# A kernel of four fused layers: in the slots of routed experts, the low part of each prepared weight piece is stored one slot behind its high part, and the second weight load is issued two slots later

## The reference, cut to what matters

```
x = x + tanh(g_xattn[0]) * retention(layernorm(x), ctx)                      # stage 1
x = x + tanh(g_ffn[0])   * (routed(x') + shared(x'))        # x' = layernorm(x), stages 2 to 4
      logits = x' @ gate_w; the 2 best of 8 experts, softmax over the two
      routed: gelu(x' @ w1[e] + b1[e]) @ w2[e] + b2[e], weighted;  shared: the same form, all tokens
x = x + tanh(g_xattn[1]) * fp8_attention(layernorm(x), ctx, wq, wqx, wk, wv, w_kv_x, ...)  # stage 5
x = x + tanh(g_ffn[1])   * dense_ffn(layernorm(x), ...)                       # stage 6
```

## Time and profile before

| | |
|---|---|
| median of 3 runs | 1681.28 us (1679.48 to 1681.79) |
| the profiled execution's own time | 1685.41 us |
| its span, first to last instruction | 1683.7 us |
| mean granted TensorE clock | 0.993 |
| PE / PEld busy | 1626.0 us (97%) / 1334.5 us (79%) |
| DVE / ACT / POOL busy | 64% / 66% / 29% |
| DMA | 220.72 MB, mean 131 GB/s |
| the slots | from about 226 us to 398 us |

### The profile page before, as it was taken

One profiled execution on the slowest core, in us unless ns is written; L12 is line 12 of the kernel. 1 busy time (PEld: TensorE's weight loads), 2 busy tenths in 40 slices (PEclk: granted clock), 3 DMA queues, 4 the chain that ended last, 5 costly groups with the idle time before them and its releaser, 6 DMA issues.

```text
span 1683.7 us, 27163 instructions
## 1 busy us (share of the span) xinstructions
PE 1626.0 (97%) x9136; PEld 1334.5 (79%) x9136; DVE 1084.2 (64%) x2115; ACT 1105.8 (66%) x2983; POOL 488.2 (29%) x515
## 2 busy tenths in 40 slices
PE   7989979999999999999999999999999999999998
PEld 6878756666778888888888888788888788887887
DVE  6258845443996668777787776666666666788322
ACT  4364245553468988888888888787787787885100
POOL 1001123222524243343342432433433334331000
PEclk9999979999999999999999999999999999999999
DMA  7031638885773242373333353121152131110011
GB/s 270 26 107 51 256 133 299 302 302 177 262 238 119 82 161 84 132 294 125 132 139 130 132 224 121 56 89 56 49 201 102 39 113 56 38 45 1 25 38 38
DMA packets 75156, 220.72 MB, mean 131 GB/s; under 512 B 6368, under 2 KB 14560, under 8 KB 68640
## 3 DMA queue, kind: packets, MB, share of 16 engines
q1 hardware_dynamic: 69360, 200.61, 32.7%
q0 software_dynamic: 5680, 18.62, 3.6%
HBM read 158.65 MB, written 60.56 MB: 130 GB/s over the span
## 4 chain that ended last, share of the span: by engine, by line
PE 72%; DMA 6%; DVE 5%; ACT 4%; issue 1%; POOL 1%; ACTq 0%; DVEq 0%; POOLq 0%; SPq 0%
PE bank L2485 10%; PE bank L2486 10%; PE bank L2548 7%; PE bank L97 6%; PE bank L99 6%; PE bank L98 6%; PE bank L2566 6%; PE bank L2579 6%; DMA s_rows<-x_rows,t_tok 5%; PE bank L2537 5%; PE bank L2558 3%; PE bank L1396 2%; PE bank L1416 2%; DVE x_res L1754 1%; PE bank L1376 1%
## 5 line engine op out<-in xcount | busy, mean ns | idle before, releaser
L2817 DVE TENSOR_TENSOR t_hn<-bank,t_rs 128x256 f32<-128x256 f32 (+1 forms) x256 | 130.8, 553 | 138.7 <-POOL t_rs L2450 73.2
L2485 PE MATMUL bank<-t_slot,t_x_q 128*128 128x512 f32 x512 | 205.8, 402 | 0.0
L2447 POOL TENSOR_SCALAR t_ve<-t_ss 128x4 f32<-128x4 f32 (+1 forms) x128 | 26.1, 204 | 615.5 <-DVE t_ss L2813 608.0
L2486 PE MATMUL bank<-t_slot,t_x_q 128*128 128x512 f32 x512 | 200.3, 391 | 0.0
L2706 ACT ACTIVATE t_sc<-bank,t_mx 128x128 f32<-128x128 f32 x512 | 184.4, 456 | 3.2 <-DVE t_mx L2837 3.2
L2450 POOL TENSOR_TENSOR t_rs<-t_ve,t_mhalf 128x4 f32<-128x4 f32 (+1 forms) x128 | 171.2, 1337 | 10.7
L2706 ACT ACTIVATION_READ_ACCUMULATOR t_sc<-bank,t_mx 128x1 f32 x512 | 151.8, 296 | 0.0
L2744 ACT ACTIVATE t_y<-bank,smooth 128x128 bf16<-128x128 f32 x512 | 139.7, 402 | 1.9 <-PE bank L2566 1.9
L2548 PEld LDWEIGHTS bank<-t_hT 128*128 128x128 f32 x1024 | 120.0, 191 | 17.0 <-ACT t_hT L2733 16.5
L2548 PE MATMUL bank<-t_hT 128*128 128x128 f32 x1024 | 131.0, 281 | 2.3 <-ACT t_hT L2733 2.3
L2486 PE MATMUL bank<-t_slot,t_x_kv 128*128 128x256 f32 x512 | 125.6, 283 | 0.0
(11 more groups left out here) (344 smaller groups left out, 4165.5 us busy)
## 6 DMA issues: line engine op xcount, KB each, us to landing
t_slot<-w_ready SPq DMA_DIRECT2D x16, 2048.0 KB, 9.3
t_xh<-xq_scratch SPq DMA_DIRECT2D x64, 512.0 KB, 3.6
t_cr<-in_ctxT_dram SPq DMA_DIRECT2D x64, 256.0 KB, 2.7
y_rows<-s_y SPq DMA_DIRECT2D x39, 256.0 KB
e_w<-in_w_units_dram SPq DMA_DIRECT2D x8, 1024.0 KB, 12.2
w_rows<-in_w_qkv_dram SPq DMA_DIRECT2D x8, 1024.0 KB, 6.2
w_ready<-w_hi SPq DMA_DIRECT2D x8, 1024.0 KB, 5.0
w_ready<-w_lo SPq DMA_DIRECT2D x8, 1024.0 KB
```

The costliest lines, as they stand in the source:

```text
L2485: nc.tensor.matmul(out, x_in[:, k, :], w[0][:, k, a:b], start=k == 0, stop=False)
L2486: last = nc.tensor.matmul(out, x_in[:, k, :], w[1][:, k, a:b], start=False, stop=k == KT - 1)
L2817: nc.vector.tensor_tensor(hn[:, lo:hi, :], b3[bk][:, 0:hi - lo, :], rs[:, lo:hi].unsqueeze(2).broadcast_to([P, hi - lo, P]), ALU.mult).the ...
```

## The change

It touches only the order in which SP issues DMAs among the slots. No instruction of another engine changes.

- `store` is taken apart into `store_hi` and `store_lo`, which move from the subclass to the base class.
- The high part of piece n is stored behind the y store of slot 4n+4, as before. The low part is stored behind the y store of slot 4n+5.
- The load of piece 1 is taken from ahead of the slots and issued behind the y store of slot 2, by the same rule as the later pieces.

```diff
-    def store(self, sp, n):
-        quarter, k = self.where(n)
-        for part, (ready, tile, stored) in enumerate(((self.hi_in, self.hi, self.hi_st),
-                                                      (self.lo_in, self.lo[n % len(self.lo)], self.lo_st[n % 2]))):
-            sp.wait_ge(ready, n + 1)
-            sp.dma_start(self.dram[quarter, :, :, part, k, :].rearrange("s p n -> p s n"),
-                         tile[:].bitcast(FP32).rearrange("p (s n) -> p s n", s=4)).then_inc(stored, 16)
+    def store_hi(self, sp, n):
+        quarter, k = self.where(n)
+        sp.wait_ge(self.hi_in, n + 1)
+        sp.dma_start(self.dram[quarter, :, :, 0, k, :].rearrange("s p n -> p s n"),
+                     self.hi[:].bitcast(FP32).rearrange("p (s n) -> p s n", s=4)).then_inc(self.hi_st, 16)
+
+    def store_lo(self, sp, n):
+        quarter, k = self.where(n)
+        sp.wait_ge(self.lo_in, n + 1)
+        sp.dma_start(self.dram[quarter, :, :, 1, k, :].rearrange("s p n -> p s n"),
+                     self.lo[n % len(self.lo)][:].bitcast(FP32).rearrange("p (s n) -> p s n", s=4)).then_inc(self.lo_st[n % 2], 16)
...
         ready.load(sp, 0)
-        ready.load(sp, 1)
         for s in range(SLOTS_N):
             sp.wait_ge(self.y_in, s + 1)
             sp.dma_start(self.env.dram["y_rows"][s * P:(s + 1) * P, :], self.y[s % 2][:]).then_inc(self.y_st[s % 2], 16)
             if s % 4 == 0 and 0 < s // 4 <= ready.count:
-                ready.store(sp, s // 4 - 1)
-            if s % 4 == 2 and 0 < s // 4 and s // 4 + 1 < ready.count:
+                ready.store_hi(sp, s // 4 - 1)
+            if s % 4 == 1 and 0 < s // 4 <= ready.count:
+                ready.store_lo(sp, s // 4 - 1)
+            if s % 4 == 2 and s // 4 + 1 < ready.count:
                 ready.load(sp, s // 4 + 1)
             if s == 4 * ready.count - 2:
                 self.units.load_shared(sp, ready, 0)
```

More of the change, by code:

```diff
@@ L213, in stored @@
             eng.wait_ge(self.lo_st[i], 16 * (count // 2))
-    def store_hi(self, sp, n):
-        quarter, k = self.where(n)
[L217 to L225, removed]
     def sums(self, dve, n):
```

## The result

The changed kernel takes 1674.9 us (median of 6, 1673.18 to 1676.25) against 1680.99 us (median of 6). The ratio is 0.9952, 95% interval 0.9938 to 0.9967; by that the change is worth 8.1 us, by the two medians 6.1. Two later comparisons with fresh runs of both gave 0.9965 (0.9945 to 0.9984) and 0.9965 (0.9951 to 0.9979), that is about 6 us. The profiled execution took 1675.36 us, its span is 1673.7 us. The forecast was 1670.1, in a range of 1668.3 to 1677.0: the measured median lies in the range and 4.8 us above the forecast.

What follows compares the result with a forecast made beforehand. The prediction took TensorE to bound the kernel, kept waiting in the slots by late gathers. 6.7 us from the loop plus 4.5 from the start made 11.2 less: 1681.3 - 11.2 = 1670.1 us, range 1668.3 to 1677.0.

Steps and rivals of the forecast that it cites:

- rival A: In the loop: the gather waits at SP's loads stay, half of 7.7 us; 8.3 us less, 1673.0 us; chance 0.18.
- What bounds the slots: Slots 5 to 38: TensorE loses 7.7 us because gathers stand behind the stores and loads SP issued around them.
- One store in front instead of two: In the loop: a gather with one 1 MB store ahead takes 5.6 us instead of up to 8.50, inside 7.3.
- The full rate: DMA engines among the slots: 357 GB/s is their full rate, so a 1 MB store takes 2.9 us.
- Of the loop's 7.7 I expect 6.7 back: Slots 5 to 38: 6.7 of 7.7 us lost return, 1.0 us left for straggling transfers; bounds 3.9 and 7.7.
- part one: In the loop: storing the low part one slot later lets gathers land in time, 6.7 us won.
- The start: First slots: moving piece 1's load removes a 2.7 us gather wait and 1.9 us of lower clock; 4.5 us taken.
- The slack of the next piece: SP waits 0.4 to 2.8 us at each load; VectorE's slack is +4.9 to -1.0 us, middle +2.2, cost zero.
- B: Gather latency hangs on volume, not order, so only the start is won; about 1677.9 us; chance 0.09.
- C: Slower: SP's load waits for the low store and VectorE's centring comes late; 1690 us; chance 0.04.
- D: The change does little, gathers straggle for other reasons; within 3 us of before, 1679.5 us; chance 0.07.
- The rule against it: Skill's rule: each DMA engine serves queues with work one packet each, so gathers get their share whatever SP has queued.

Runs made afterwards that it cites:

- e5: The kernel before, with each store of a prepared piece cut to its first quarter (256 KB instead of 1 MB): ratio 0.9959 to before.
- e9: The changed kernel, with each store of a prepared piece cut to its first quarter (256 KB): 1674.13 us, ratio 0.9939 to before.
- e1: The kernel before again, with no edit, for a second profile: 1683.59 us against 1682.97, ratio 1.0005.
- e3: The kernel before with only the low part stored one slot later, pieces 0 and 1 both loaded ahead of the slots: ratio 0.9982 to before.
- e4: The changed kernel again, with no edit, for a second profile: 1676.23 us, ratio 0.9965 to before.
- e2: The kernel before with only the load of piece 1 moved behind slot 2, both parts still stored together: 1679.02 us, ratio 0.9977 to before.
- e10: The changed kernel once more, with no edit, for a third profile: ratio 0.9965 to before.
- e8: The changed kernel with the word of experts loaded by TensorE's sequencer one slot earlier: 1674.77 us, ratio 0.9948 to before.
- e6: The changed kernel with the low part of each of the first eight pieces stored twice: 1691.32 us, ratio 1.0046 to before.
- e7: The changed kernel with the load of piece n+1 behind the y store of slot 4n+3 instead of 4n+2: 1675.04 us, ratio 0.9954 to before.

## Why the prediction came out as it did

- **The number.** The median of 1674.9 us is inside the range, but not inside the likeliest case's 1668.8 to 1672; it is nearer to rival A's 1673.0 than to the forecast's 1670.1. By medians 6.1 of the 11.2 us came, by the first ratio 8.1. Turns 5 to 38 took 137.5 us, not the 136.5 at most that was to show the forecast.
- **What bounds the slots.** Right. Taking away three quarters of the stores' bytes takes the loop loss to zero (e5, e9).
- **One store in front instead of two.** Right in kind: with the same bytes the loop lost 6.6 to 8.8 us in four profiles with the parts together and 0.9 to 3.9 in seven with them apart.
- **The full rate.** The sum takes 357 GB/s for every transfer. With the 16 engines full, stores alone moved 340 (1.70 MB in 5 us), and loads with a gather 427 (e1, 232 to 235 us). By these rates, 1 MB is some 3.1 us of store or 2.5 of load, where the sum has 2.9 for both. That shifts its latencies by a few tenths.
- **"Of the loop's 7.7 I expect 6.7 back."** This is the term that was mis-sized. Over three profiles each, the loop loses (7.9 + 8.8 + 6.6) / 3 = 7.8 us before and (2.1 + 0.9 + 3.9) / 3 = 2.3 us after: 5.5 us back. By timed runs part one is worth 3.0 us (e3's ratio) or 2.8 (e4 under e2). I had left 1.0 us for stragglers. What the runs showed in its place: a gather beside the low store can take 7.90 us (e10), not 5.8; a gather behind a late load 7.50 and 7.84; and the word's load takes up to 1.2 us, which I had not looked for. The sum had said that a load which waits for its low part costs TensorE nothing, as it goes out behind the gather of its slot. It can go out so late that it meets the gather of the next one.
- **The start.** 4.5 us forecast, 4.6 in the first pair of profiles, 0.0 lost in every kernel with the change. But the loss that it removes was 4.6, 2.0 and 4.4 us in three executions of before and 1.9 in e3, and the timed worth is 3.9 (e2). The wait was rightly read. I took its length, and with it the clock's fall, as certain from one trace.
- **The slack of the next piece.** Right. SP's wait was forecast at 0.4 to 2.8 us and measured at 2.1 on average, 2.5 at most; no wait of VectorE for a load in the changed kernel's first profile, one of 0.4 us in e10 and one of 0.8 in e8. The low part's landing had a median of 6.1 us, where I had taken 5.0 from the high stores.
- **Nothing given back behind the slots.** Right: 1299.0 and 1299.4 us follow the last turn, and the means of three profiles each are both 1300.0.
- **The rivals.** A happens in part: in e10 TensorE waited for gathers three times in the loop, and gathers behind a late load are in its chain. B falls with the eleven profiles named at e3. C came only with 3 MB of stores for each piece instead of 2 (e6). D falls: none of the three intervals allows no gain, and two of them lie above 3 us.
- **The rule against it.** By the Trainium skill's round-robin (DMA: Bandwidth & Descriptors, section Queues, rings and completion order) the gather would not stand behind a store. The changed kernel's rows show 2 packets of the gather's queue beside 605 of SP's, so this trace does not agree in that stretch either; in the two microseconds behind it they show 80 beside 263. Why the gather stands is not shown.

The forecast of 11.2 us was nearer to the pair of profiles (10.0) than to the timed medians (6.1). Over three profiles each, the losses in the slots differ by 3.7 us at the start and 5.5 us in the loop, 9.2 of the 9.8 us between the means of the profiled times. The timed medians differ by about 6. The three profiled executions of before lay 4.4, 4.8 and 0.0 us above the median of their comparison, those of the changed kernel 0.5 above and 1.8 and 0.6 below: that makes the 3.7 us of difference. Three profiles of each are too few to say whether chance made it.

## What to carry to other kernels

A small transfer that an engine waits for, beside large ones that nobody waits for, is late by what is issued in one go around it and not by the mean load: keep large transfers a slot apart when the bytes fit, and check with the large ones cut short how much there is to win at all. Before pricing a stall from one trace, ask whether the next execution has it, above all the part of it that is a lower clock. When a load is moved behind a wait, compare its landing with when its data are used, and the y buffers' stores behind it too.

## What I had not expected of the hardware

The executions of the kernel before lie between 1678 and 1691 us. What its three profiles differ by could be placed in the stretch before the slots (227.6 to 230.1 us), the losses in the slots (10.8 to 12.5) and the rest (1299.0 to 1301.5). The gathers of 256 KB that TensorE waited for took 7 to 9 us; one ahead of the slots, at 217.44 in the first profile, took 3.54. A register load from SBUF by TensorE's sequencer took 0.3 us in the loop with small stores (e5, e9) and up to 1.4 us in the loops with whole ones (e7), though not in all of them.
